# Causal attention rows taken in pairs, and the next group's projections moved among the last rows of the turn before

## The reference, cut to what matters

```python
h   = layernorm(x) * (1 + ca) + sa
qkv = einsum('bsh,ph->bsp', h, weight_qkv)            # per group: 4 q heads, 1 k, 1 v, each 128 wide
scores = where(causal, einsum('bsgqd,btgd->bgqst', q, k) / sqrt(128), min)
out = einsum('bgqst,btgd->bsgqd', softmax(scores), v)
x   = x + ga * (out.reshape(b, s, 2048) @ weight_proj.T)
h   = layernorm(x) * (1 + cb) + sb
x   = x + gb * ffn(h)       # two Walsh-Hadamard transforms, gate/up to 1024, silu, down to 256
```

## Time and profile before

| | |
|---|---|
| profiled execution | 979.04 us, span from first to last instruction 977.2 us |
| PE matmul busy | 947.1 us (97%), 5344 matmuls |
| DVE busy | 653.1 us (67%) |
| ACT busy | 516.6 us (53%) |
| POOL busy | 467.7 us (48%) |
| granted TensorE clock, mean | 0.997 |
| first chunk of turn 0 starts | 24.66 us |
| first chunk of turns 1, 3, 4 starts | 128.68, 326.49, 425.25 us |
| the feed-forward part's first matmul starts | 820.36 us |

### The profile page before, as it was taken

How to read it: one execution, slowest core, us unless ns; L and a number is a source line. 1 busy time by engine, 2 the same in 40 slices (tenths; PEclk the granted TensorE clock), 3 DMA queues, 4 the chain that set the end, 5 groups by cost and what they waited for, 6 DMA issues and landing times.

```text
span 977.2 us, 14506 instructions
## 1 busy us (share of the span) xinstructions
PE 947.1 (97%) x5344; PEld 816.0 (83%) x5344; DVE 653.1 (67%) x1290; ACT 516.6 (53%) x1085; POOL 467.7 (48%) x603
## 2 busy tenths in 40 slices
PE   6899999999999999999999999999999999999997
PEld 5688888888898889888988898889888987888885
DVE  6777657775777577757775777567757776864553
ACT  2466646664666466646664666466646665331221
POOL 3665646564556455545654565456545656120000
PEclk9999999999999999999999999999999999999999
DMA  8000000100010001000000010001000020000000
GB/s 313 24 1 33 2 22 1 33 1 22 1 33 2 22 1 33 1 23 1 33 1 22 1 33 1 22 1 34 1 1 1 1 87 1 1 8 15 21 21 21
DMA packets 9666, 21.92 MB, mean 22 GB/s; under 512 B 1280, under 2 KB 5504, under 8 KB 9472
## 3 DMA queue, kind: packets, MB, share of 16 engines
q1 hardware_dynamic: 8736, 20.45, 6.2%
q10 hardware_dynamic: 864, 0.60, 0.2%
HBM read 18.96 MB, written 2.10 MB: 22 GB/s over the span
## 4 chain that ended last, share of the span: by engine, by line
PE 80%; DVE 9%; ACT 5%; POOL 3%; issue 2%; DMA 1%; SPq 0%; DVEq 0%; POOLq 0%; ACTq 0%
PE ps L801 17%; PE ps L803 16%; PE ps L802 16%; PE ps L924 10%; PE ps L903 6%; PE ps L909 6%; PE ps L906 6%; ACT prob L487 2%; POOL rinv L373 2%; DVE pt_lo L706 2%; POOL prob L378 2%; DVE xhat L614 1%; DVE ps L702 1%; PE ps L825 1%; DVE v_lo L681 1%
## 5 line engine op out<-in xcount | busy, mean ns | idle before, releaser
L706 DVE TENSOR_TENSOR pt_lo<-ps,pt_hi 128x512 fp32r<-128x512 f32 x288 | 198.0, 690 | 101.7 <-ACT pt_hi L506 98.9
L506 ACT ACTIVATE pt_hi<-ps 128x512 fp32r<-128x512 f32 x288 | 171.0, 597 | 134.1 <-PE ps L924 132.6
L373 POOL TENSOR_TENSOR rinv<-rsum,mone 128x1 f32<-128x1 f32 x256 | 140.7, 550 | 211.5 <-ACT prob L487 210.7
L378 POOL TENSOR_SCALAR prob<-prob,rinv 128x1024 f32<-128x1024 f32 (+7 forms) x256 | 192.2, 751 | 53.3 <-POOL rinv L373 53.3
L487 ACT ACTIVATE prob<-ps,nmax 128x1024 f32<-128x1024 f32 (+7 forms) x256 | 189.5, 741 | 50.0 <-DVE nmax L702 48.3
L702 DVE CUSTOM_DVE_ANT_0 ps<-ps,mask_f 128x1024 f32<-128x1024 f32 (+7 forms) x256 | 192.9, 765 | 21.8 <-PE ps L909 19.5
L924 PE MATMUL ps<-ident,prob 128*128 128x128 f32 x1152 | 175.1, 273 | 6.2 <-DVE pt_lo L706 3.6
L924 PEld LDWEIGHTS ps<-ident,prob 128*128 128x128 f32 x1152 | 140.3, 140 | 36.8 <-DVE pt_lo L706 10.9
L801 PE MATMUL ps<-pt_hi,v_hi 128*128 128x512 f32 x288 | 132.5, 460 | 1.3 <-DVE pt_lo L706 0.5
L803 PE MATMUL ps<-pt_hi,v_lo 128*128 128x512 f32 x320 | 126.3, 395 | 0.0
L903 PE MATMUL ps<-k_hi,q_hi 128*128 128x512 f32 (+4 forms) x384 | 117.6, 360 | 0.0
(11 more groups left out here) (134 smaller groups left out, 1575.8 us busy)
## 6 DMA issues: line engine op xcount, KB each, us to landing
w_raw<-in_wqkv SPq DMA_DIRECT2D x9, 768.0 KB, 4.2
wp_raw<-in_wproj SPq DMA_DIRECT2D x8, 512.0 KB, 3.5
x<-in_x SPq DMA_DIRECT2D x4, 512.0 KB, 9.8
prob<-in_wug SPq DMA_DIRECT2D x4, 512.0 KB, 5.3
out_y<-prob SPq DMA_DIRECT2D x4, 512.0 KB, 3.0
prob<-in_wmod SPq DMA_DIRECT2D x1, 1024.0 KB, 9.7
raw_down<-in_wdn SPq DMA_DIRECT2D x1, 1024.0 KB, 14.1
prob<-in_wmod SPq DMA_DIRECT2D x1, 512.0 KB, 5.2
```

Of the source, the lines that this page charges most:

```text
L378: g_.tensor_scalar(row, row, rinv[:, s % 2, h:h + 1], 1.0, ALU.mult, ALU.mult).then_inc(prob_done, 1)
L506: a_.activation(pt_hi[:, n % 3, :], T[n % 2], ACT.Copy).then_inc(pth_done, 1)
L706: v_.tensor_tensor(pt_lo[:, n % 3, :], T[n % 2], pt_hi[:, n % 3, :].bitcast(F32), ALU.subtract).then_inc(ptl_done, 1)
```

## The change

Row blocks go in pairs, called windows: (7, 0), (6, 1), (5, 2), (4, 3), nine units each: three units of the big row, all of the small one, then the rest of the big one. The two rows' scores for the next window are spread over a window's units, one to a unit. The last window has no scores to spread; there the 12 chunks of the next turn stand (order k, k, q of the second half, v, v, q of the first half), in the four banks of the score tensors, and layernorm's front part. What neither fits there stands at the head of a turn: the scores of rows 7 and 0, the last `Y` of the turn before (row 4), VT, L and S6 0. For turn 0 all 12 chunks stand ahead of its head. On POOL the split of the projection weights (`WP`) goes behind the normalising of row 7, their scaling (`WM`) into the third window of the turn before, `ln_low` (`LL`) behind row 0, the split of the qkv weights (`W`) into the second window. `v` has a buffer of its own before it is transposed, probabilities of the small row lie behind those of the big one, the output accumulators' banks and the waits follow the new order.

```diff
-STEPS = [NT - 1 - s for s in range(NT)]
-UNITS = [(i, j) for i in STEPS for j in range(i + 1)]
+WINDOWS = [(NT - 1 - p, p) for p in range(NW)]
+HEAD = 3
+for big, small in WINDOWS:
+    UNITS += [(big, j) for j in range(HEAD)] + [(small, j) for j in range(small + 1)] + [(big, j) for j in range(HEAD, big + 1)]
+SCORED = [i for pair in WINDOWS for i in pair]
+FINISHED = [i for big, small in WINDOWS for i in (small, big)]
-    out = [("C", 0, 0), ("C", 1, 0), ("C", 2, 0), ("C", 3, 0), ("VT", 0, 0), ("C", 4, 0), ("C", 5, 0), ("L", 0, 0)]
-    for h in range(QPG):
-        out += [("S", STEPS[0], h), ("C", 6 + h, 0)]
-    out += [("C", 10, 0), ("S", STEPS[1], 0), ("C", 11, 0)]
...
+CHUNKS = [("k", 0, 0), ("k", 0, 1)] + [("q", h, 1) for h in range(QPG)]
+CHUNKS += [("v", 0, 0), ("v", 0, 1)] + [("q", h, 0) for h in range(QPG)]
+LAG = 2
+    out = [(0, "LF", 0, 0)] + [(0, "C", c, 0) for c in range(NC)]
+    for t in range(TURNS):
+        last = [(t - 1, "Y", WINDOWS[-1][0], 0)] if t else []
+        s7, s0, s6 = scores(t, NT - 1), scores(t, 0), scores(t, NT - 2)
+        out += s7[:1] + last + [s7[1], (t, "VT", 0, 0), s7[2], (t, "LN", 0, 0), s7[3], (t, "L", 0, 0)]
+        out += [(t, "WP", 0, 0)] * (t > 0) + s0 + [(t, "LL", 0, 0)] + s6[:1]
+        behind, due = [], []
+        def value():
+            n = behind.pop(0)
+            out.append((t, "V", n, 0))
+            if due and due[0][0] == 1:
+                out.append((t, "Y", due.pop(0)[1], 0))
+            for row in due:
+                row[0] -= 1
+            if n == LAST[UNITS[n][0]]:
+                due.append([2, UNITS[n][0]])
+        for p, pair in enumerate(WINDOWS):
+            units = [n for n, u in enumerate(UNITS) if u[0] in pair]
+            fill = [[] for _ in units]
+            if p + 1 < NW:
+                for k, item in enumerate([item for i in WINDOWS[p + 1] for item in scores(t, i)][p == 0:]):
+                    fill[k].append(item)
+            elif t + 1 < TURNS:
+                for c in range(NC):
+                    fill[c * len(units) // NC].append((t + 1, "C", c, 0))
+                fill[4].append((t + 1, "LF", 0, 0))
+            if p in (1, 2) and t + 1 < TURNS:
+                fill[3].append((t, "W", 0, 0) if p == 1 else (t + 1, "WM", 0, 0))
+            for n, extra in zip(units, fill):
+                out += extra[:1] + [(t, "T", n, 0)] + extra[1:]
+                behind.append(n)
+                if len(behind) > LAG:
+                    value()
+        while behind:
+            value()
...
-        prob = sb("prob", [P, 2, QPG, SEQ])
+        prob = sb("prob", [P, 2, QPG, SEQ + P])
...
         def bank(c):
-            return psum[c // 2][:, c % 2 * CH:(c % 2 + 1) * CH] if c < 4 else X[c % 2]
+            return S[c % 4 // 2][:, c % 2 * CH:(c % 2 + 1) * CH]
...
+                if c >= 4:
+                    pe.wait_ge(*evicted(t, c - 4))
...
-                            if e < QPG:
-                                pe.wait_ge(qkv_lo, this(qkv_lo, t, 3 + e))
-                            if e >= 2:
-                                pe.wait_ge(exp_done, this(exp_done, t, e - 1 if n >= CT or n == CT - 1 and h < 2 else e - 3))
+                    e = scored(n, h)
+                    if e <= 2:
+                        for c in (NC - 4, NC - 3) if e == 1 else (NC - 2, NC - 1):
+                            pe.wait_ge(*evicted(t, c))
+                    else:
+                        pe.wait_ge(exp_done, this(exp_done, t, e - 2 if n >= CT or h < 2 else e - 4))
```

More of the change, by code:

```diff
@@ new lines, with window, scores @@
+CHUNKS = [("k", 0, 0), ("k", 0, 1)] + [("q", h, 1) for h in range(QPG)]
+CHUNKS += [("v", 0, 0), ("v", 0, 1)] + [("q", h, 0) for h in range(QPG)]
+NC = len(CHUNKS)
+LAG = 2
+def window(i):
+    return min(i, NT - 1 - i)
+def walk():
+    out = [(0, "LF", 0, 0)] + [(0, "C", c, 0) for c in range(NC)]
+    def scores(t, i):
+        return [(t, "S", i, h) for h in range(QPG)]
+    for t in range(TURNS):
[32 more added lines that the diff above has]
+            value()
+        assert [i for _, i in due] == [WINDOWS[-1][0]]
+    return out + [(TURNS - 1, "Y", WINDOWS[-1][0], 0)]
@@ L178, in build @@
         X = [psum[3][:, 0:CH], psum[3][:, CH:2 * CH]]
-        O = [X[s % 2] for s in range(NT - 1)] + [psum[1][:, CH:2 * CH]]
+        O = [X[(window(i) + (i < CT)) % 2] for i in range(NT)]
         x_in_s = [sem(f"x_loaded{c}") for c in range(NC_B)] + [sem("x_loaded_rest")]
@@ L352, in _ @@
             pool.wait_ge(gate_ok, 1)
[L353 to L387, removed]
@@ new lines, in normalise @@
+            def normalise(t, i, h):
+                e = scored(i, h)
+                at = place(i)
+                pool.wait_ge(exp_done, this(exp_done, t, e))
+                g_.tensor_tensor(rinv[:, at, h:h + 1], rsum[:, at, h:h + 1], mone[:, :], ALU.pow).then_inc(rinv_done, 1)
+                pool.wait_ge(rinv_done, this(rinv_done, t, e))
+                pool.sem_inc(pool_gate, 1)
+                g_.tensor_scalar(row(i, h), row(i, h), rinv[:, at, h:h + 1], 1.0, ALU.mult, ALU.mult).then_inc(prob_done, 1)
@@ new lines, in _ @@
+            scale_wp(0)
+            split_wp(0)
+            for t, what, n, h in WALK:
+                if what == "LF":
+                    ln_rstd(1, t // NKV, t % NKV, 0)
+                if what == "S":
+                    normalise(t, n, h)
+                if what == "LL":
+                    ln_low(1, t // NKV, t % NKV, 0)
+                if what == "W":
+                    pool.wait_ge(wraw_s, (t + 2) * 16)
+                    pool.wait_ge(qkv_done, this(qkv_done, t, 12))
+                    split_w()
+                    pool.wait_ge(w_hi_s, t + 2)
+                    g_.tensor_tensor(w_lo[:, :, :], w_raw[:, :, :], w_hi[:, :, :].bitcast(F32),
+                                     ALU.subtract).then_inc(w_ready, 1)
+                if what == "WM":
+                    scale_wp(t)
+                if what == "WP":
+                    split_wp(t)
@@ L455, in _ @@
             act.wait_ge(small_s, 5 * 16)
[L456 to L494, removed]
-                            if n == 3:
-                                v_high()
-                            exps()
-                        if what == "L":
-                            ln_modulate(1, b, g, 0)
-                        if what == "S":
-                            exps()
-                            waiting.append((n, h))
-                        if what == "T":
-                            act.wait_ge(t_done, this(t_done, t, n + 1))
-                            a_.activation(pt_hi[:, n % 3, :], T[n % 2], ACT.Copy).then_inc(pth_done, 1)
-                            exps()
-                        if what == "V" and n == LAST[UNITS[n][0]]:
-                            s = NT - 1 - UNITS[n][0]
-                            act.wait_ge(pv_done, this(pv_done, t, n + 1))
-                            a_.activation(o_hi[:, s % 2, :], O[s], ACT.Copy).then_inc(oh_done, 1)
@@ new lines, in v_high, with chunk @@
+            def v_high(t):
+                for n in range(2):
+                    act.wait_ge(vtr_done, this(vtr_done, t, n + 1))
+                    a_.activation(v_hi[:, 4 * n:4 * n + 4, :].rearrange("p j d -> p (j d)"), T[n], ACT.Copy).then_inc(v_hi_s, 1)
+            def chunk(t, c):
+                what, h, half = CHUNKS[c]
+                act.wait_ge(qkv_done, this(qkv_done, t, c + 1))
+                span = slice(half * CH, (half + 1) * CH)
+                if what == "v":
+                    a_.activation(vt[:, span], bank(c), ACT.Copy).then_inc(vt_done, 1)
+                elif what == "k":
+                    a_.activation(k_hi[:, span], bank(c), ACT.Copy).then_inc(qkv_hi, 1)
+                else:
+                    a_.activation(q_hi[:, h, span], bank(c), ACT.Copy, scale=SCALE).then_inc(qkv_hi, 1)
@@ new lines, in _, with exps @@
+            waiting = []
+            def exps():
+                while waiting:
+                    t, i, h = waiting.pop(0)
+                    nb, w = halves(i)
+                    act.wait_ge(max_done, this(max_done, t, scored(i, h)))
+                    a_.activation(row(i, h).rearrange("p (a n) -> p a n", a=nb),
+                                  score_banks(i, h).rearrange("p (a n) -> p a n", a=nb)[:, :, 0:w],
+                                  ACT.Exp, bias=nmax[:, place(i), h:h + 1], scale=-1.0,
+                                  accum_out=rsum[:, place(i), h:h + 1]).then_inc(exp_done, 1)
@@ new lines, in _ @@
+            for t, what, n, h in WALK:
+                if what == "C":
+                    chunk(t, n)
+                    exps()
+                if what == "VT":
+                    v_high(t)
+                if what == "L":
+                    ln_modulate(1, t // NKV, t % NKV, 0)
+                if what == "S":
+                    exps()
+                    waiting.append((t, n, h))
+                if what == "T":
```

(30 more changed lines are left out.)

328 lines of the change are left out of this document (149 added, 179 removed).

## The result

The kernel after takes 1033.88 us (median of 4 runs, 1032.98 to 1034.87), the kernel before 979.16 beside it (977.29 to 979.96): 1.0562 times as long, 95% interval 1.0544 to 1.058. The forecast of 1013.0 had the sign; the time lies above its range, 998 to 1026. The profiled execution took 1033.74 us, span 1032.0, mean granted clock 0.972 (before: 979.04, 977.2, 0.997).

A forecast was written before the change was run, and what follows sets the result against it. PE bounds the kernel by its waits: a steady turn 98.8 - 2.9 + 5.3 + 1.1 + 0.4 = 102.7 us, +3.9; seven give +27, turn 0 +5.5; 979.04 + 32.5 = 1011.5, one clock fall makes 1013. Range 998 to 1026.

The forecast's parts named there:

- What bounds it: Whole kernel: PE sets the pace, its instructions stay the same, so all turns on where PE waits.
- the thirteen places: Steady turn: items taking too long on PE in thirteen places, together 2.9 us, which the change would remove.
- the drain: Turn's end: the last unit's V still waits for ACT and DVE; 0.4 us stays.
- The head's walk: Turn's head, without chunks as cover: PE waits 0.8 (S7 3), 0.75 (L), 3.05 (S0 1), 0.7 (S6 0), 1.1 (S6 2).
- I put one in: Heads: whether the clock falls behind 3 us standstills was undecided; one fall was counted, taking 1011.5 to 1013 us.
- at most 1.7: Heads: the most one clock fall costs, in us, less where PE would have waited anyway.
- Rival 3: Every head: the clock falls, seven times up to 1.7 us, giving 1023 us; chance 25%.
- Turn 0: First turn: PE stands 4.4 us for k_lo behind four chunks, clock falls 1.7; 104.0 becomes 109.5 us, +5.5.
- POOL at nothing: Steady turn: POOL has row 0 ready at 23.2, asked for at 23.3, so its lateness was costed at nothing.
- rival 2: Row 0 or row 1: POOL decides, two us late in seven turns, giving 1025 us; chance 13%.
- Rival 1: Head: exp 3 (row 7's last exponential) not behind the modulations, or exponentials drained under other work; change wins, 960 us; chance 7%.
- 5.3 + 1.1 + 0.4: Steady turn's expected waits in us: the head up to S6 0, then S6 2, then the turn's end.

The follow-up runs named there:

- a_pairs_only: Kernel after with e3's POOL order, rows in pairs, but the 12 chunks at their own turn's head, interleaved with row 7's scores as before: 984.68 us.
- a2: a_pairs_only with chunk 10 ahead of row 0's first score, chunk 11 right behind it, and row 6's second score a unit later: 979.5 us.
- e2: Kernel after with 12 matmuls of 512 columns that nobody reads added on PE between row 0's first and second scores: 1020.33 us.
- e3: Kernel after with turn 0's projection-weight scaling and splitting on POOL put back behind the layernorm step: 1030.05 us.
- e1: Kernel after with the exponential of row 7's last score put ahead of L's four modulations on ACT: 1024.8 us.
- b: Kernel after with e3's POOL order and four of the twelve chunks back between row 7's scores, eight left in the last window: 999.87 us.
- d: b reordered: last Y and VT behind row 7's second score, four chunks behind its last, L behind row 0 with e1's edit, window items later: 1005.92 us.
- a5: a_pairs_only with v's chunks last, among row 0's scores, and VT behind row 6's first score: 985.29 us.

## Why the prediction was wrong

- **What bounds it; the thirteen places.** Right: PE, and all depended on its waits. Those in rows 7 to 0 went, 0.34 + 0.11 at the drain were left (0.4 predicted). a_pairs_only and a2 show what the step left out: the pairs bring row 0's scores into the head, and these and the first of row 6 wait 2 to 3 us there even with all chunks beside them.
- **The head's walk.** Right in place and nearly in size: S7 3 0.63 (0.8 predicted), S0 1 2.99 (3.05, behind the modulations), S6 0 0.74 (0.7) where e2 kept the clock up, S6 2 0.96 (1.1). L waited 1.15, not 0.75: xhat lasted 1.54 instead of 1.26, beside a busy POOL. That POOL is the cause was not tried, and before, POOL was busy beside xhat too. In all the walk gave 6.4 us and measured 6.5, the miss of L and the smaller ones of S7 3 and S6 2 in part cancelling.
- **"I put one in": the clock.** This step failed: the fall was counted in one head and came in all eight. A standstill of 2.84 us with 1.3 us of waits ahead was enough each time; that this is shorter than 3.7 was no evidence that the clock would hold. The price was right on average by luck: "at most 1.7" came from one fall of 3.4 us, while six of the eight lasted 6.8 to 6.9 us and the five of them in steady turns cost 1.7 to 2.2; the short ones cost 1.0 to 1.1 (e2: mean 1.7). Rival 3, at 25%, is what happened; its 1023 took the head and turn 0 as walked. The Trainium skill ("TensorE: Matmul & The Clock Gate", HAM oscillation — how this bites in real kernels) tells of a kernel whose clock fell at each wait for data, so that each tile began cold. The trace agrees that the fall comes back every time, with clock 0.50 behind the gap and 1.7 us a head; the waits that the section tells of, 3 to 5 us, are longer than the 2.84 that did it here.
- **Turn 0.** The 4.4 us took DVE's first k_lo at its time of before. The change moves POOL's weight work ahead of it, and POOL had been costed for steady turns alone: this step failed too. 8.03 measured; e3's edit brings it to 4.28 and the kernel down by 3.8 us. The Trainium skill ("GPSIMD Engine Reference", 1. Specifications) says that GpSimd and VectorE share their way into SBUF and contend in some kinds of instruction; the trace agrees, with 2.34 us beside POOL and 0.17 without; whether DVE's instruction is of such a kind no trace shows.
- **POOL at nothing (rival 2).** Right in the steady turn: PE waits for nothing from POOL at row 0 or 1.
- **Rival 1** was wrong: e1 took exp 3 from behind the modulations, and the turn still held 6.8 us of waits.

The account, by waits over clean distances: a steady turn holds 9.0 on average instead of 6.8 (5.3 + 1.1 + 0.4), seven times 2.24 or 15.7 us, 11.7 of them the clock by e2; the other 4.0, 0.6 a turn, were not traced to a cause. Turn 0 holds 19.7 instead of 13.5, 6.2 us more, of which 3.6 are the longer standstill and at least 0.9 the clock in its head. Less the 1.5 us that the sum had for one fall, these are 20.4 of the 20.7 us between 1013 and the profiled 1033.74.

Open is why the orders of the head each gave less than was worked out for them: the misses were found one at a time in the traces, each an eviction or exponential behind an item that its engine had to take first, but not one of them was undone alone.

## What to carry to other kernels

Work that gives a stretch no wait of its own can still be the cover of another: before moving it, walk the stretch that it leaves, all engines in list order. Once the walk leaves PE waits of some 3 us close together, count the clock's fall in every turn, not once: it fell in all eight heads with 2.84 us in one piece, in five of seven steady heads with two gaps of 1.1 to 1.5 us (e1, b), in four with one of 1.9 us (d), and in none where the longest was 1.1 or 1.3 us (a_pairs_only, a5). And price a moved step on the engines beside it at its new place, the first turn too.

## What was not expected of the hardware

- PE's clock went to 1.2 GHz behind a standstill of 2.84 us, and with gaps of 1.4 and 1.5 us (e1) in five of seven steady heads, while the other two, with the same gaps, kept 2.4 GHz. It stayed there for 3.4 or 6.8 to 6.9 us.
- 12 useless matmuls in a gap made the kernel 13.6 us faster (1033.88 to 1020.33).
- A DVE operation on 128x4 elements takes 2.34 us when it starts with a POOL instruction of 2.34 us, 0.17 alone.
